# Six relations instead of five by Strassen's scheme, with PSUM banks seeded by ScalarE, in a graph network and mixture-of-experts kernel

## What is computed

```
h = layernorm(x)
u = h @ root + bias
for r in range(8):                     # eight relations
    mean_r = segment_mean(h[src] where edge_type == r, dst)
    u = u + mean_r @ weight[r]         # weight[r]: 1024 x 1024
z = concat(u, h) @ w_gate + b_gate
x = x + tanh(u) * z + h * (1 - z)
```

## Time and profile before

| what | value |
|---|---|
| median of three runs | 1109.83 us |
| the profiled execution, own time | 1113.76 us |
| its span, first to last instruction | 1112.0 us |
| TensorE busy | 1066.2 us (96%) |
| VectorE busy | 793.0 us (71%) |
| ScalarE busy | 413.9 us (37%) |
| GpSimd busy | 417.4 us (38%) |
| units 1 to 8 and the root on TensorE | about 14 to 499 us of the span |
| spreading | 499 to 685 us |

### The profile page before, as it was taken

The page is one execution under the profiler, slowest core; times in us unless marked ns, Lnnn a source line. Parts: engine busy times, 40 slices in busy tenths (PEclk is TensorE's granted clock), DMA queues, the critical chain, the costliest instruction groups (busy, mean ns, idle before and its releaser), DMA issues.

```text
span 1112.0 us, 14475 instructions
## 1 busy us (share of the span) xinstructions
PE 1066.2 (96%) x5385; PEld 891.4 (80%) x5385; DVE 793.0 (71%) x1591; ACT 413.9 (37%) x647; POOL 417.4 (38%) x272
## 2 busy tenths in 40 slices
PE   6998999999999999999999998999979999999995
PEld 5776887777787777889999998887756878888774
DVE  7567888889989897317667776495479648876647
ACT  3331333434434343122332323361443415256652
POOL 6023488788788888212442330000010000410016
PEclk9999999999999999999999999999989999989998
DMA  9999978788977776799999742523242201588757
GB/s 322 400 331 383 327 181 145 193 218 208 223 193 147 196 140 161 169 244 219 271 261 252 170 126 99 208 83 126 60 80 89 76 2 59 223 281 277 235 180 258
DMA packets 94475, 217.34 MB, mean 195 GB/s; under 512 B 29978, under 2 KB 46173, under 8 KB 85947
## 3 DMA queue, kind: packets, MB, share of 16 engines
q1 hardware_dynamic: 39488, 137.19, 36.5%
q0 software_dynamic: 37504, 48.18, 21.8%
q10 hardware_dynamic: 17406, 30.97, 10.1%
HBM read 149.59 MB, written 66.71 MB: 195 GB/s over the span
## 4 chain that ended last, share of the span: by engine, by line
PE 78%; DVE 10%; DMA 6%; ACT 3%; issue 1%; ACTq 1%; POOLq 0%; SPq 0%; DVEq 0%
PE ps L583 65%; PE ps L891 3%; PE ps L928 3%; DVE rl L414 3%; DVE EQ L1578 3%; DMA stage<-in_w_e 2%; PE ps L855 2%; DMA stage<-in_w_rel 2%; DMA KR<-key_scratch 2%; PE ps L573 1%; ACT rh L405 1%; DVE V L1498 1%; ACT He L1106 1%; PE ps L939 1%; PE ps L906 1%
## 5 line engine op out<-in xcount | busy, mean ns | idle before, releaser
L2219 POOL DMA_INDIRECT adj_scratch<-cnt,idx x164 | 288.9, 1762 | 133.8 <-issue 43.6
L414 DVE TENSOR_TENSOR rl<-stage,rh 128x512 fp32r<-128x512 f32 (+1 forms) x264 | 213.4, 837 | 152.3 <-ACT rh L405 148.7
L405 ACT CAST rh<-stage 128x512 fp32r<-128x512 f32 (+1 forms) x264 | 180.4, 716 | 364.9 <-PE ps L583 242.8
L583 PE MATMUL ps<-rh,xTh 128*125 128x512 f32 x600 | 239.0, 398 | 5.7 <-ACT He L1106 4.6
L583 PE MATMUL ps<-rl,xTh 128*125 128x512 f32 x600 | 237.5, 396 | 0.0
L583 PE MATMUL ps<-rh,xTl 128*125 128x512 f32 x600 | 237.4, 396 | 0.0
L583 PE MATMUL ps<-rh,Ar 125*125 125x342 f32 x600 | 190.8, 323 | 5.4 <-issue 4.0
L583 PE MATMUL ps<-rl,Ar 125*125 125x342 f32 x600 | 190.3, 322 | 0.0
L583 PEld LDWEIGHTS ps<-rh,xTh 128*125 128x125 f32 x600 | 112.0, 187 | 35.9 <-ACT He L1106 7.2
L583 PEld LDWEIGHTS ps<-rh,xTl 128*125 128x125 f32 x600 | 112.1, 187 | 28.4
L583 PEld LDWEIGHTS ps<-rl,xTh 128*125 128x125 f32 x600 | 112.0, 187 | 27.4
(11 more groups left out here) (295 smaller groups left out, 1615.1 us busy)
## 6 DMA issues: line engine op xcount, KB each, us to landing
stage<-in_w_rel SPq DMA_DIRECT2D x22, 1024.0 KB, 6.4
stage<-h_scratch SPq DMA_DIRECT2D x24, 855.0 KB, 7.3
stage<-in_w_e SPq DMA_DIRECT2D x16, 1024.0 KB, 6.6
adj_scratch<-Z POOLq DMA_DIRECT2D x16, 767.0 KB, 20.1
adj_scratch<-Z SPq DMA_DIRECT2D x16, 767.0 KB, 16.1
h_scratch<-He ACTq DMA_DIRECT2D x40, 257.0 KB, 9.1
h_scratch<-He ACTq DMA_DIRECT2D x40, 256.0 KB, 4.7
KR<-key_scratch ACTq DMA_DIRECT2D x37, 256.0 KB, 6.5
```

What stands on the lines that cost most here:

```text
L405: e.copy(h, s).then_inc(*a_hi.up(*[("hi", t) for t in step(i)]))
L414: e.tensor_tensor(l, s, h.bitcast(F32), ALU.subtract).then_inc(*v_lo.up(*[("lo", t) for t in step(i)]))
L583: ins = e.matmul(ps[0:P, b, 0:width], a, m, start=first and n == 0, stop=last and n == len(parts) - 1, skip_group_check=again)
L2219: e.indirect_dma_start(accd[to], bass.IndirectOffsetOnAxis(ap=idx[:, n:n + 1], axis=0), cnt[:, n:n + 1], None, compute_op=ALU.add).then_in ...
```

## The change

It makes unit 3 a fast unit and shifts what goes before it. The S pieces are made during the two halves of unit 2 (before: second half of unit 2, first half of unit 3). The first half of unit 2 has three key windows instead of six, unit 3's halves have none, and each of the six fast units has five instead of four. Inside a fast unit, ScalarE writes a copy of W into the banks of X, the negative of X into those of Z, and the negative of chunk 4's first product into its second bank (`seed`), and TensorE's matmuls then add to what stands there (`start` is false for them). ScalarE also makes V2 and V3 by plain copies, and copies the last three output blocks, all of which VectorE did by additions. The buffer V5 goes.

```diff
-WINDOWS = {(0, 1): (0, 2, 4, 6), (1, 0): (0, 1, 2, 4, 5, 6), (1, 1): (0, 2, 4), (2, 0): (2, 4, 6), (2, 1): (0, 2, 4, 6),
+WINDOWS = {(0, 1): (0, 2, 4, 6), (1, 0): (0, 2, 4), (1, 1): (0, 2, 4),
            (8, 0): (), (8, 1): ()}
-FAST = (4, 5, 6, 7, 8)
+FAST = (3, 4, 5, 6, 7, 8)
+SEEDED = (("X", 0), ("X", 1), ("Z", 0), ("Z", 1), ("E", 2))
-KEYS_IN_FAST = {u: (3, 10, 17, 24) for u in FAST}
-S_IN = ((1, 1), (2, 0))
+KEYS_IN_FAST = {u: (2, 8, 13, 18, 24) for u in FAST}
+S_IN = ((1, 0), (1, 1))
@@ tensor, part() of fast_unit
+                    seeded = role in SEEDED
                     on.wait_ge(*at("lo", i))
-                    for ev in (*ready, *(old if start else ())):
+                    if start and seeded:
+                        before_seed[u, role] = old
+                        on.wait_ge(*at("seed", u, role))
+                    for ev in (*ready, *(old if start and not seeded else ())):
                         on.wait_ge(*at(*ev))
-                    return three(b, i, stat, start, stop, kind in ("t4", "b21", "b22"))
+                    return three(b, i, stat, start and not seeded, stop, seeded or kind in ("t4", "b21"))
@@ scalar
+            def seed(u, role, source, sign, ready):
+                to, b = (ps[0:P, banks.of["fast", u, *name], :] for name in (role, source))
+                on.wait_ge(*at(*ready))
+                for ev in before_seed[u, role]:
+                    on.wait_ge(*at(*ev))
+                e.activation(to, b, ACT.Copy, scale=sign).then_inc(*a_out.up(("seed", u, role)))
+
             def fast_between(i):
                 for u in FAST:
                     if i - F0[u] == 13:
                         for p in range(2):
-                            e.copy(V2[0:P, p, :], ps[0:P, banks.of["fast", u, "W", p], :]).then_inc(*a_out.up(("v1", u, p)))
-                        e.copy(V5[0:P, :], ps[0:P, banks.of["fast", u, "E", 1], :]).then_inc(*a_out.up(("v5", u)))
+                            seed(u, ("X", p), ("W", p), 1.0, ("fast", u, "b11", ("W", p)))
+                    if i - F0[u] == 17:
+                        for p in range(2):
+                            e.copy(V2[0:P, p, :], ps[0:P, banks.of["fast", u, "X", p], :]).then_inc(*a_out.up(("v2", u, p)))
+                            seed(u, ("Z", p), ("X", p), -1.0, ("fast", u, "t2", ("X", p)))
+                        seed(u, ("E", 2), ("E", 1), -1.0, ("fast", u, "b11", ("E", 1)))
+                    if i - F0[u] == 21:
+                        for p in range(2):
+                            e.copy(V3[0:P, p, :], ps[0:P, banks.of["fast", u, "Y", p], :]).then_inc(*a_out.up(("v3", u, p)))
...
-                    if i - F0[u] == 39:
+                    if i - F0[u] == (36 if u == FAST[-1] else 37):
+                        for p in range(2):
+                            h_copy(u, 2 * p, 1, banks.of["fast", u, "Z", p], "fast", u, "b22", ("Z", p))
+                        h_copy(u, 4, 1, banks.of["fast", u, "E", 2], "fast", u, "b22", ("E", 2))
                         for c in (0, 2, 4):
                             h_store(u, c, 1)
@@ vector, fast_before: the steps at 17, 21 and 37 go (seven additions), those at 25 and 29 stay
```

More of the change, by code:

```diff
@@ L224, in gnn_ffn_kernel @@
         He = sb("He", [128, NHE, 514], F32, ph0)
-        V5 = sb("V5", [128, 512], F32, phx)
-        phx.close()
         er = [sb(f"er{i}", [128, 2, 128], I32, ph0) for i in range(3)]
@@ L312, in gnn_ffn_kernel @@
         banks = Banks()
+        before_seed = {}
         groups, tiles, tile, vacant, latest = [], [], {}, [], {}
@@ L660, in fast_unit @@
                 for p in range(2):
-                    held["X", p] = banks.take(("fast", u, "X", p), ("v2", u, p), where=of.get(("X", p)))
+                    held["X", p] = banks.take(("fast", u, "X", p), ("v2", u, p), ("seed", u, ("Z", p)), where=of.get(("X", p)))
                 for p in range(2):
@@ L686, in fast_unit @@
                     for p in range(2):
-                        ends(part("b21", j, ("W", p), x_stat(4 + j, 2 * p), False, j == 3, ("v1", u, p)), "b21", j, ("W", p), ("E", 1))
-                    ends(part("b21", j, ("E", 1), x_stat(4 + j, 4), False, j == 3, ("v5", u)), "b21", j, ("E", 1), ("E", 1))
+                        ends(part("b21", j, ("W", p), x_stat(4 + j, 2 * p), False, j == 3, ("seed", u, ("X", p))), "b21", j, ("W", p), ("E", 1))
+                    ends(part("b21", j, ("E", 1), x_stat(4 + j, 4), False, j == 3, ("seed", u, ("E", 2))), "b21", j, ("E", 1), ("E", 1))
                 for j in range(4):
@@ L1437, in fast_before @@
                 for u in FAST:
-                    if i - F0[u] == 17:
-                        for p in range(2):
-                            on.wait_ge(*at("fast", u, "t2", ("X", p)))
-                            on.wait_ge(*at("v1", u, p))
-                            e.tensor_tensor(V2[0:P, p, :], ps[0:P, banks.of["fast", u, "X", p], :], V2[0:P, p, :], ALU.add).then_inc(*v_out.up(("v2", u, p)))
-                    if i - F0[u] == 21:
-                        for p in range(2):
-                            on.wait_ge(*at("fast", u, "t3", ("Y", p)))
-                            on.wait_ge(*at("v2", u, p))
-                            on.wait_ge(*at("s lo", 1, 1))
-                            if u != FAST[0]:
-                                on.wait_ge(*at("he", u - 1, 2 * p + 1, 1))
-                            e.tensor_tensor(V3[0:P, p, :], ps[0:P, banks.of["fast", u, "Y", p], :], V2[0:P, p, :], ALU.add).then_inc(*v_out.up(("v3", u, p)))
                     if i - F0[u] == 25:
@@ L1456, in fast_before @@
                             h_made(u, 2 * p + 1, 0, banks.of["fast", u, "Y", p], V2[0:P, p, :], ALU.add, ("fast", u, "t4", ("Y", p)), ("v2", u, p))
-                    if i - F0[u] == (36 if u == FAST[-1] else 37):
-                        for p in range(2):
-                            h_made(u, 2 * p, 1, banks.of["fast", u, "Z", p], V2[0:P, p, :], ALU.subtract, ("fast", u, "b22", ("Z", p)), ("v2", u, p))
-                        h_made(u, 4, 1, banks.of["fast", u, "E", 2], V5[0:P, :], ALU.subtract, ("fast", u, "b22", ("E", 2)), ("v5", u))
             def fast_after(i):
@@ L2242, in pool @@
                 on.wait_ge(*at("added", NG - 1))
-                for c in (0, 2, 4):
-                    on.wait_ge(*at("he", FAST[-1], c, 1))
+                for c in (1, 3):
+                    on.wait_ge(*at("he", FAST[-1], c, 0))
                 for j in range(4):
```

12 lines of the change are left out of this document (6 added, 6 removed).

## The result

The changed kernel takes **1122.03 us** (median of 4 runs, 1120.75 to 1123.77), the kernel before in the same comparison 1109.88 us. The ratio is 1.0109 with a 95% interval of 1.0089 to 1.0128: slower by 12.2 us. The forecast was 1123.7 us, 13.9 more than before. The profiled execution of the changed kernel has an own time of 1121.96 us, at the median; that of the kernel before lay 3.9 us above its median, so the two spans differ by only 8.2 us.

The account below looks back on a forecast made before the run. TensorE, busy 1066.2 of 1112.0 us, was taken as the bound. Unit 4's t2 13.4 us later, with 5.6 us fewer matmuls and 3 us won included, plus 0.5 for seeds, gave 1109.83 + 13.9 = 1123.7 us, range 1111 to 1130.

Parts of the forecast that it names:

- Fewer matmuls: Unit 3 on TensorE goes from 240 to 216 matmuls, at 0.232 us each 5.6 us less.
- First half of unit 2: VectorE drops three windows and gains S pieces; TensorE's stop shrinks from 4.1 to about 2.1 us, 3 us won.
- The loads: Second half of unit 2: VectorE's sums wait behind queued zeros for b12 until 118 us and b22 until 133.
- From b22 to the seeds: Before unit 3's t2: VectorE's chain takes 21.9 us, then ScalarE's copies, roundings and first seed; TensorE may begin at 163.6.
- The clock: After TensorE's stop before unit 3's t2, about 8 matmuls run at half speed, costing 1.6 us once.
- Seeds in the later units: TensorE waits 0.1 us for seeds in each of five later units, 0.5 us; bounds 0 and 1.3 each.
- Sum: First t2 of unit 4 at 215.3 against 201.87, 13.4 us later; 13.9 with seeds, total 1123.7 us.
- the signs: Expected in the trace: first Sx at 160 to 166 us, idle 18 to 22, VectorE waiting for stageC, t2 50.1 to 50.4 apart.
- Lighter wait for loads: Before unit 3: blocks come in time, only VectorE's work delays seeds; stop of 11 us, total 1113.7; chance 0.15.
- Seeds late in every unit: In the fast units each seed ends 1.3 us after TensorE wants it, 6.0 us more, total 1129.7; chance 0.12.
- Faster: Before unit 3: seeds come before 142.5 us, so TensorE never stops; total 1100.6; chance 0.08.

Follow-up runs that it names:

- both moved: Changed kernel with block loads issued earlier among the writes of zeros and unit 2's three second-half windows moved to units 4 to 6: 1103.30 us, ratio 0.9950.
- experiment with additions: Changed kernel's plan of six relations, windows, S pieces and keys, but VectorE's additions as before in place of seeds: 1120.12 us, ratio 1.0079.
- "both moved" with additions: The plan of "both moved" with VectorE's additions in place of the seeds: 1111.25 us, ratio 1.0021.
- both loads ahead: "both moved" plus ScalarE's copies of unit 2's first half earlier, and the b22 and b21 loads ahead of all eight zero writes: 1103.49 us, ratio 0.9919.
- five relations: Kernel before with seeds, its five relations kept, three windows of unit 2's first half moved to units 4 to 6: 1111.55 us, ratio 1.0013.
- windows later: Changed kernel with the three windows of unit 2's second half moved to units 4, 5 and 6: 1119.44 us, ratio 1.0064.

## Why the prediction was right

**Fewer matmuls, 5.6 us.** As said: 24 matmuls fewer, 50.1 us per unit.

**First half of unit 2.** Forecast: load 8 there at 104.4, first copy at 107.5, stop of 2.1 us. Measured: the tile of load 8 is rounded from 102.78 on, the first copy starts at 105.97, the stop is 2.45 us. Everything is 1.5 us early, the stop nearly as said. The change didn't bring these 1.5 us. Up to the start of unit 2 both programs do the same work, but in the two profiled executions TensorE began unit 2 at different times, first the kernel before, then the changed one:

```profile
74.72 0.39 PE L583 MATMUL ps<-rh,xTh 128*125 128x512 f32 x1
```

```profile
73.16 0.39 PE L583 MATMUL ps<-rh,xTh 128*125 128x512 f32 x1
```

In the kernel before the first ten matmuls on weights took 4.3 us (from 14.02 on), in the changed one 2.5 us. All times of the forecast were worked out from an execution that was 1.6 us late.

**The loads.** b12 forecast for 118, bounds 114 and 123; measured 114.76. b22 forecast for 133, bounds 121 and 136; measured 130.12. Both are about 3 us early, at one distance, so it is one term. The late execution is 1.6 us of it. For the rest, with the first half shorter, SyncE issued load 9 at 100.95 instead of 109.53, and I had kept the landing of the zeros behind it where it was. The first of them landed at 116.98, and at 121.1 before. That zeros stand ahead was the right cause: with b22 in front of them it is there at 111.3.

**From b22 to the seeds.** 21.9 us forecast for VectorE's chain, 151.87 - 130.12 = 21.8 measured. ScalarE behind it 8.7 forecast, 160.39 - 151.98 = 8.4 measured. The seed's price, taken as 0.6 us, was bounded by 0.53 and 0.7 us: two seeds take 1.06, as two copies do. The rule of the Trainium skill ("ScalarE: Activation LUTs", Step-by-step: what each stage is for) that PSUM is the faster destination is not borne out by these rows.

**The clock.** 1.6 us forecast from a stop of 4 us; 13 matmuls at 0.43 instead of 0.23 us cost 2.5. From t2 of unit 3 to that of unit 4 it is 213.02 - 160.39 = 52.6 us. This term was 0.9 too small.

**Seeds in the later units, 0.5 us.** Measured nothing: the first seed of unit 4 ends at 212.4, TensorE wants it at 213.02.

**Sum.** Forecast for t2 of unit 4: 13.4 us later. Measured: 213.02 - 201.87 = 11.15; t2 of unit 3 came 3.2 us earlier than forecast, and the clock puts 0.9 on. Counted from TensorE's start of unit 2 it is 12.7 us. Behind unit 8 I had put nothing, and there the two profiled executions differ by 3 us the other way: 1.4 us at the start of the spreading, 1.2 us behind a branch (stops of 0.76 and 2.04 us instead of 4.00), both in the last section, and small things. So the spans differ by 8.2 us. The measured medians differ by 12.2 us, 9.9 to 14.2 by the interval. How much of the 3 us is in the medians, one execution of each kernel can't tell, so it is partly luck that the total came out within 1.7 us. The stop and what it is made of, 17.6 us against the 21 forecast, is not: the experiments took it apart. Of the signs, the first Sx at 160 to 166 us, VectorE's wait for stageC and 50.1 us per unit came. The stop is just under the 18 to 22 us, the last He copy of unit 2 came at 156.64 and not after 159, and the profile doesn't name the seed.

**The rivals.** *Lighter wait for loads* had its condition met by 3 us of 10, half of them by the late execution. The rule on completion order that spoke for it ("DMA: Bandwidth & Descriptors", Queues, rings and completion order, of the Trainium skill) shows in no landing here: the last zeros landed at 116.98, 119.83, 123.42 and 126.28, and VectorE had b22 at 130.12. *Seeds late in every unit* fell. *Faster* needed VectorE's last S operation by about 134 us; "both moved" has it at 133.5 and TensorE hardly stops, so that was the right threshold for the wrong kernel. It gives 1103.3, not the 1100.6 of that rival.

**What I had not separated.** I counted ScalarE's 8.7 us as part of a chain, and that was right; but I didn't say that 7 of them exist only because t2 waits for a seed. The experiment with additions showed it, and my expectation for it was wrong in just this.

## What to carry to other kernels

Moving work off a busy engine pays only where the freed time is used: by the traces seeds were worth nothing with four windows per unit, 1.7 us in six units with five (from the first t1 to the last 250.5 us, with additions 252.2), and 6.7 us with six in three of them. Against that stood 7 us once, in front of the first fast unit. Before a stage is pulled forward, follow its operands back to the queue that brings them: cheap writes that nobody waits for stood in front of two loads on which a 21.8 us chain hung. And the first pass through a pipeline has other neighbours than the steady one: a two-microsecond producer placed behind five copies costs what stands in front of it, once.

## What the runs showed of the hardware

**VectorE and GpSimd.** At the start of the spreading stage VectorE's low part of 125x1710 takes 1.94 us in the three kernels in which GpSimd's addition of 128x3125 starts 0.94 us or more behind its own start. In the ten others that addition starts between 4.01 us ahead of it and 0.76 us behind it, and VectorE's operation takes 4.13 to 8.91 us. Kernel before, and "both moved" with additions:

```profile
501.38 7.51 DVE L414 TENSOR_TENSOR rl<-stage,rh 125x1710 fp32r<-125x1710 f32 x1 [1.04 <-ACT rh L405]
...
500.75 6.34 POOL L2237 TENSOR_TENSOR Atot<-Atot,Ar 128x3125 f32<-128x3125 f32 x1
```

```profile
499.96 1.94 DVE L414 TENSOR_TENSOR rl<-stage,rh 125x1710 fp32r<-125x1710 f32 x1 [1.04 <-ACT rh L405]
...
500.90 6.59 POOL L2238 TENSOR_TENSOR Atot<-Atot,Ar 128x3125 f32<-128x3125 f32 x1
```

In all ten VectorE's operation ends 1.80 to 1.81 us behind the end of GpSimd's, as if it had begun only then. TensorE stood still for 0.6 to 2.8 us behind it in seven of them (1.44 in the kernel before, nothing in the changed one, whose GpSimd came earlier). That is 1.4 of the 3 us by which the two profiled spans differ less than the starts of t2 do. By the Trainium skill ("SBUF — State Buffer", SBUF: two separate sides) the two share a pair of ports, which one of them holds for a whole instruction while the other waits. The fixed 1.8 us behind GpSimd's end agree; that the one which starts first gets it does not quite: GpSimd went first also where it started up to 0.76 us later by the profile. No kernel here took GpSimd's addition away; when GpSimd begins depends on a load of the adjacency, so this may also be a part of the scatter between runs.

**A branch.** Behind the conditional jump of the spreading stage VectorE does nothing for 1.0 us in every kernel with six relations and seeds, and for 3.3 to 4.2 us in the others, the kernel before among them:

```profile
690.29 3.10 DVE L414 TENSOR_TENSOR rl<-stage,rh 128x512 fp32r<-128x512 f32 x5 [3.34 <-issue]
```

```profile
697.42 3.10 DVE L414 TENSOR_TENSOR rl<-stage,rh 128x512 fp32r<-128x512 f32 x5 [1.04 <-issue]
```

TensorE's stop there is 2.04 and 4.0 to 5.2 us; all but the kernel before have one of 0.76 us just ahead of it as well. The cause stays open; the code at that place is the same in all of them, its distance from the start of the program isn't. A comparison of totals between six relations with seeds and with additions has up to 3.1 us of this in it, for which no run shows that the seeds are the cause.

**The clock after a stop.** Windows of the changed kernel and of "both loads ahead" (busy time of PE, PEld, DVE, ACT, POOL, then the granted clock):

```profile
160.00:165.00 5.00, 4.61 (x11) 3.65 (x12) 4.93 (x14) 1.92 (x4) 4.39 (x3) 0.50 0.38 31
```

```profile
140.00:145.00 5.00, 4.32 (x19) 3.51 (x20) 4.93 (x14) 2.84 (x6) 4.39 (x3) 1.00 0.59 39
```

Behind a stop of 17.58 us the granted clock is 0.50, 1.2 GHz; behind one of 2.27 us it is 1.00, 2.4 GHz. In front of unit 3 the stops of 4.85 to 17.58 us cost 1.5 to 2.5 us on top (from the first t2 to the first t1 it is 34.9 to 35.9 us instead of 33.4), without growing with the length: 4.85 us cost 2.3, 9.46 us 1.6, 17.58 us 2.5. Those of 0.80 and 2.27 us cost nothing. Length alone doesn't decide it: the stop of 1.86 us with five relations was followed by a mean clock of 0.66, and in the first half of unit 2 a stop of 2.45 us was followed by a mean clock of 0.68 in the changed kernel, and one of 3.01 us by 1.00 with the windows later:

```profile
106.00:111.00 5.00, 4.31 (x11) 3.14 (x12) 0.02 (x1) 2.90 (x6) 3.80 (x3) 0.68 1.01 422
```

```profile
106.00:111.00 5.00, 4.87 (x20) 3.61 (x21) 0.00 (x0) 2.80 (x5) 3.48 (x3) 1.00 1.02 427
```

By the Trainium skill ("TensorE: Matmul & The Clock Gate", Part 1: The HAM clock gate) an idle engine goes back to half its clock. That fits the long stops here; stops of up to 3 us came out either way. One price for a stop of any length, as the forecast had it, held for the long ones.
